# Perceiver block with soft mixture of experts on one core: score order, row fetches, turned logit rows and turning banks rearranged

## What is computed

```
x = x + xattn(layernorm(x), ctx)   # cross attention, width 256, softmax over 4096 keys, then Wo
x = x + attn(layernorm(x))         # causal self attention, 16 heads of 16; heads 0 to 2 weighted by region
x = x + ffn(layernorm(x))          # soft mixture of experts: 64 experts, 32 slots each

# ffn
logits = x @ phi.T + b             # 1024 tokens x 2048 slots
D = softmax(logits, over the 32 slots of an expert)
C = softmax(logits, over the 64 experts)
X = clip(D.T @ x); X = tanh(norm(X)); Y = X @ expert_w + expert_b
out = C @ Y
```

## Time and profile before

| | us |
|---|---|
| three runs | 563.71, 567.41, 567.92 |
| median | 567.41 |
| profiled execution, own time | 567.7 |
| its span in the profile | 565.9 |
| TensorE busy in the span | 533.9 |
| VectorE, ScalarE, GpSimd busy | 363.3, 363.8, 361.7 |

### The profile page before, as it was taken

How to read it: one execution, slowest core, us unless ns; L and a number is a source line. 1 busy time by engine, 2 the same in 40 slices (tenths; PEclk the granted TensorE clock), 3 DMA queues, 4 the chain that set the end, 5 groups by cost and what they waited for, 6 DMA issues and landing times. The chain is left out here.

```text
span 565.9 us, 9355 instructions
## 1 busy us (share of the span) xinstructions
PE 533.9 (94%) x3256; PEld 414.5 (73%) x3256; DVE 363.3 (64%) x736; ACT 363.8 (64%) x1016; POOL 361.7 (64%) x282
## 2 busy tenths in 40 slices
PE   5898999999999999999898989889999999899998
PEld 4786888888888888777566656446555887578898
DVE  1785344564455345745776898686999998588340
ACT  2446765856584866873787886328999895666320
POOL 2775989659775784755559675243465899688500
PEclk9999999999999999999898999999999999999999
DMA  8463464675743733175139500400000643978110
GB/s 295 160 224 134 163 224 162 185 282 183 251 149 131 248 143 103 48 169 136 32 100 204 181 1 1 151 0 1 1 1 1 118 105 109 331 230 245 57 48 28
DMA packets 38669, 75.45 MB, mean 133 GB/s; under 512 B 3408, under 2 KB 27360, under 8 KB 37728
## 3 DMA queue, kind: packets, MB, share of 16 engines
q1 hardware_dynamic: 36864, 68.57, 39.6%
q10 hardware_dynamic: 1760, 6.30, 3.1%
HBM read 68.56 MB, written 6.30 MB: 132 GB/s over the span
## 5 line engine op out<-in xcount | busy, mean ns | idle before, releaser
L387 POOL TENSOR_TENSOR ctxT_lo<-front,ctxT_hi 128x1024 fp32r<-128x1024 f32 x32 | 76.9, 2408 | 46.2 <-ACT ctxT_hi L682 46.2
L503 PE MATMUL ps<-ctx_both,pT_hi 128*128 128x512 f32 x256 | 94.6, 409 | 1.9 <-DVE pT_lo L858 1.9
L392 POOL TENSOR_TENSOR ctx_both<-ctx_in,ctx_both 128x1024 fp32r<-128x1024 f32 x32 | 76.5, 2395 | 16.3 <-ACT ctx_both L687 16.3
L505 PE MATMUL ps<-ctx_both,pT_lo 128*128 128x256 f32 x256 | 71.9, 281 | 0.0
L1774 PE MATMUL ps<-front,turned 128*128 128x512 f32 x128 | 61.0, 605 | 0.3 <-PEq L1008 0.3
L850 DVE TENSOR_SCALAR_CACHE_REDUCE first<-ps,qbk 128x512 f32<-128x512 f32 x32 | 24.0, 750 | 55.5 <-PE ps L475 53.2
L706 ACT CAST pT_hi<-ps 128x512 fp32r<-128x512 f32 x64 | 34.0, 590 | 38.3 <-PE ps L487 38.3
L503 PEld LDWEIGHTS ps<-ctx_both,pT_hi 128*128 128x128 f32 x256 | 48.2, 188 | 13.1 <-DVE pT_lo L858 2.8
L858 DVE TENSOR_TENSOR pT_lo<-ps,pT_hi 128x512 fp32r<-128x512 f32 x64 | 41.1, 685 | 16.4 <-ACT pT_hi L706 16.4
L1919 ACT ACTIVATE comb<-comb,cneg 128x64 f32<-128x64 f32 x128 | 50.8, 411 | 0.0
L505 PEld LDWEIGHTS ps<-ctx_both,pT_lo 128*128 128x128 f32 x256 | 48.5, 190 | 0.1
(11 more groups left out here) (260 smaller groups left out, 1436.1 us busy)
## 6 DMA issues: line engine op xcount, KB each, us to landing
front<-in_ctx_turned_dram SPq DMA_DIRECT2D x32, 512.0 KB, 4.7
ctx_in<-in_ctx_dram SPq DMA_DIRECT2D x32, 512.0 KB, 3.5
back<-in_L_ffn_expert_w_dram SPq DMA_DIRECT2D x11, 1024.0 KB, 5.9
turned<-in_L_ffn_expert_w_dram SPq DMA_DIRECT2D x5, 1024.0 KB, 5.8
phi_piece<-in_phi_turned_dram ACTq DMA_DIRECT2D x8, 512.0 KB, 6.3
phi_less_dram<-phi_piece ACTq DMA_DIRECT2D x4, 512.0 KB, 3.1
front<-phi_less_dram SPq DMA_DIRECT2D x1, 2048.0 KB, 14.0
front<-in_L_ffn_expert_b_dram SPq DMA_DIRECT2D x4, 512.0 KB, 10.2
```

Of the source, the lines that this page charges most:

```text
L387: nc.gpsimd.tensor_tensor(ctxT_lo[:, n % RING, :, :], turned_in[:, n % SLOTS, :, :], ctxT_hi[:, n % RING, :, :].bitcast(F32), ALU.subtract ...
L392: nc.gpsimd.tensor_tensor(ctx_both[:, m % RING, :, 1, :], by_tile(m), ctx_both[:, m % RING, :, 0, :].bitcast(F32), ALU.subtract).then_inc( ...
L503: nc.tensor.matmul(pO[q][:], pT_hi[:, c % 2, q, cols], ctx_both[:, m % RING, j, :, :].rearrange("p k d -> p (k d)"), start=c == 0 and j == ...
L505: last = nc.tensor.matmul(pO[q][:, 0:D], pT_lo[:, c % 2, q, cols], ctx_both[:, m % RING, j, 0, :], start=False, stop=c == NCH - 1 and j == ...
```

## The change

1. SP: the store of piece 3 is issued at the end of the first block. In the second block the order becomes stack 2, stack 3, then for s = 4 to 7 "store s, stack s".
2. Self attention, TensorE: the scores of group 1 come before `project_v(0..2)`. VectorE: maxima of group 1 come before the values, `last_norm` between its parts 1 and 2. ScalarE: the copy of the turned normed rows moves from behind `transposed(0)` to between `exps(2, 1)` and `exps(2, 2)`.
3. Logits: `norm` of the last tiles at v = 1 in place of 2; both copies of the turned rows at v = 4 in place of 5.
4. Experts: the pieces of C for tiles 0 to 5 go round three banks (0, 1 and 5) in place of two. Bank 5 was the second bank of the turned inputs, which now have bank 4 alone, so `transpose_inputs(s)` waits for ScalarE's copy of s - 1 in place of s - 2. Tiles 6 and 7 stay with banks 0 and 1.

```diff
@@ cross_attention, sync
                 if s < 2:
                     stack_rows(sp, kept, qk_dram, q_rows, k_rows, s)
+            store_parts(sp, kept, qk_dram, parts(3), 3)
             sp.wait_ge(phi_out, 16 * (4 + 1))
@@ self_attention, sync
             stack_rows(sp, kept, qk_dram, *first_rows(kept), 2)
-            store_parts(sp, kept, qk_dram, parts_in(kept.first, 3), 3)
             stack_rows(sp, kept, qk_dram, *first_rows(kept), 3)
-            store_parts(sp, kept, qk_dram, parts[:, 0, :, :], 4)
             for s in range(4, 8):
-                if s < 7:
-                    store_parts(sp, kept, qk_dram, parts[:, s - 3, :, :], s + 1)
+                store_parts(sp, kept, qk_dram, parts[:, s - 4, :, :], s)
                 stack_rows(sp, kept, qk_dram, q_late, k_late, s)
@@ self_attention, tensor
             product_of_attended()
+            for part in range(3):
+                score(1, part)
             for s in range(3):
                 project_v(s)
-            for part in range(3):
-                score(1, part)
@@ self_attention, scalar
                     exps(i + 2, 1)
+                    if i == 0:
+                        act.wait_ge(h2T_mm, B)
+                        nc.scalar.copy(hT[:, :, LAST * S:B * S], split_halves(psX[:])).then_inc(h2T_a, 1)
                     exps(i + 2, 2)
                 ...
                 transposed(i)
-                if i == 0:
-                    act.wait_ge(h2T_mm, B)
-                    nc.scalar.copy(hT[:, :, LAST * S:B * S], split_halves(psX[:])).then_inc(h2T_a, 1)
@@ self_attention, vector
             last_sums()
+            maxima(1, 0)
+            maxima(1, 1)
+            last_norm()
+            maxima(1, 2)
             values(0)
             values(1)
-            last_norm()
+            invert_sums(1, 0)
             values(2)
-            maxima(1, 0)
-            maxima(1, 1)
-            maxima(1, 2)
-            invert_sums(1, 0)
+            invert_sums(1, 1)
             maxima(2, 0)
-            invert_sums(1, 1)
@@ soft_moe
-        psL, psT, psE, psC = bank[0:4], bank[4:6], bank[6:8], bank[0:2]
+        psL, psT, psE, psC = bank[0:4], bank[4], bank[6:8], (bank[0], bank[1], bank[5])
+        def turn_bank(c, k):
+            return psC[(LB * c + k) % 3 if c < TT - 2 else k % 2]
@@ transpose_combine
-                    at_least(pe, cTlo_v, LB * c + k - 1)
+                    at_least(pe, cTlo_v, LB * c + k - (2 if c < TT - 2 else 1))
@@ transpose_inputs
-                at_least(pe, xT_a, s - 1)
+                at_least(pe, xT_a, s)
@@ soft_moe, tensor
-                if s < 2:
-                    pe.wait_ge(clip_v, 2 * s + 2)
+                if s == 0:
+                    pe.wait_ge(clip_v, 2)
@@ soft_moe, scalar
-                if v == LB + 1:
+                if v == LB:
                     act.wait_ge(pro_mm, 2)
@@ soft_moe, vector
-                if v == 2:
+                if v == 1:
                     dve.wait_ge(rstd_g, 2)
                     norm(TT - QT, TT)
-                if v == LB + 1:
+                if v == LB:
                     dve.wait_ge(pro_mm, 1)
```

More of the change, by code:

```diff
@@ L1794, in transpose_combine @@
                     pe.wait_ge(cmul_g, LB * c + k + 1)
-                    at_least(pe, cTlo_v, LB * c + k - 1)
+                    at_least(pe, cTlo_v, LB * c + k - (2 if c < TT - 2 else 1))
                     for j in range(4):
-                        last = nc.tensor.transpose(psC[k % 2][:, j * P:(j + 1) * P],
+                        last = nc.tensor.transpose(turn_bank(c, k)[:, j * P:(j + 1) * P],
                                                    comb[:, c, (4 * k + j) * P:(4 * k + j + 1) * P], ident[:])
@@ L1802, in transpose_inputs @@
                 pe.wait_ge(tanh_a, s + 1)
-                at_least(pe, xT_a, s - 1)
+                at_least(pe, xT_a, s)
                 for c in range(DH):
-                    last = nc.tensor.transpose(psT[s % 2][:, c * P:(c + 1) * P], xh[:, s % 2, c * P:(c + 1) * P], ident[:])
+                    last = nc.tensor.transpose(psT[:, c * P:(c + 1) * P], xh[:, s % 2, c * P:(c + 1) * P], ident[:])
                 last.then_inc(xT_mm, 1)
@@ L1928, in combine_out @@
                     act.wait_ge(cT_mm, LB * c + k + 1)
-                    nc.scalar.copy(comb_hi[c][:, k * 512:(k + 1) * 512], psC[k % 2][:]).then_inc(cT_a, 1)
+                    nc.scalar.copy(comb_hi[c][:, k * 512:(k + 1) * 512], turn_bank(c, k)[:]).then_inc(cT_a, 1)
             def outputs_high(s):
@@ L1974, in _ @@
                 at_least(act, e_mm, s - 1)
-                nc.scalar.copy(xhT[:, s % 2, :, :].rearrange("p c s -> p (c s)"), psT[s % 2][:, 0:DH * P]).then_inc(xT_a, 1)
+                nc.scalar.copy(xhT[:, s % 2, :, :].rearrange("p c s -> p (c s)"), psT[:, 0:DH * P]).then_inc(xT_a, 1)
                 if turned_at(s) is not None:
@@ L2084, in combine_low @@
                     dve.wait_ge(cT_a, LB * c + k + 1)
-                    nc.vector.tensor_tensor(comb_lo[:, c, cols], psC[k % 2][:], comb_hi[c][:, cols].bitcast(F32),
+                    nc.vector.tensor_tensor(comb_lo[:, c, cols], turn_bank(c, k)[:], comb_hi[c][:, cols].bitcast(F32),
                                             ALU.subtract).then_inc(cTlo_v, 1)
```

## The result

The changed kernel took 560.47 us in the median of 4 runs (556.28 to 560.81), the kernel before beside it 565.83; the ratio is 0.9869, with a 95% interval of 0.9820 to 0.9917. So it is faster by 1.3 to 1.5%, 5.4 to 8.7 us by the medians. The profiled execution took 560.81 us, span 559.0, against 567.7 and 565.9 before. The forecast was 557.0, range 553 to 562. The sum behind it was 10.8 us, though, and the two spans differ by 6.9: this needs an account by stages. Runs in the chip's slower state are left out of all medians here: one of ten of no1, and the profiled one of sp_old_late (762 us at a mean granted clock of 0.66), which therefore has no usable trace.

The account below looks back on a forecast made before the run. TensorE was taken as the bound: 533.9 of 565.9 us at work, about 32 standing. Gains 3.1 + 0 + 5.5 + 2.2 = 10.8 from 567.7 gave 556.9 (556.6 by the median), stated as 557.0, range 553.0 to 562.0.

Parts of the forecast that it names:

- Part 2: Self attention: scores of group 1 ahead of the values start `project_qk(4)` 3.1 us earlier; ends 1.5 and 3.5.
- Part 1: SP's store order: rows 4 and 5 come without a wait, but the stall only moves; gain 0, ends 0 and 1.9.
- 1.33 + 0.62: Self attention: the stall before `score(8, 0)` moves to before L1250 and keeps this length in us.
- Part 3: Logits: turned rows a unit sooner bring `logit(10)` 5.5 us earlier; ends 2.5 and 5.9.
- the three things in the rows: Logits: a 1.35 us wait for the norm, 2.55 for the copy, 1.7 for a slow unit; together 5.6.
- the 0.3 for unit 4: Logits: TensorE would lose 0.3 us waiting for unit 4's early inputs, which want a division on GpSimd.
- The rival with VectorE as the bound: Logits: VectorE takes the place of the waits, gain there 2.5 us, total 7.8, time 559.9; chance 0.12.
- The rival of the clock: Logits: small TensorE stops lower the clock, 1.7 us more per unit; 573.9 us with ten slow units; chance 0.03.
- the stretch that I held against it: Logits, 400 to 440 us: clock 1.00 with TensorE busy 40.00 of 40 us, cited against the clock falling.
- Part 4: Experts: three banks for the pieces of C end step 7 2.2 us earlier; ends 0.5 and 2.7.
- its first two rivals: VectorE bounds the logits (559.9 us, chance 0.12); experts stay bound by ScalarE or the weights (560 us, chance 0.09).
- the lower ends: Smallest gains of the four parts; the prediction summed them to 5 to 6 us, giving 562.

Follow-up runs that it names:

- no1: The changed kernel with all SP edits undone (store 3 late, each store of 4 to 7 ahead of the stack before it); median 558.67 us.
- sp_old_late: The changed kernel with store 3 still early but stores and stacks of 4 to 7 in the old order; median 555.35 us.
- sp_7: The changed kernel with store 7 alone issued ahead of stack 6; median 555.35 us.
- no4: The changed kernel with two banks again for the pieces of C and two for the turned inputs; median 561.78 us.
- new_again: The changed kernel run once more, unchanged; median 557.87 us, ratio 0.9851 to the kernel before.
- no2: The changed kernel with group 1's scores behind the values again, ScalarE's copy and VectorE's order also undone; median 559.42 us.
- warm: The changed kernel with twenty transposes of the identity on TensorE ahead of its first weights; median 555.24 us.
- no3: The changed kernel with the turned rows of the logits a unit later again; median 561.95 us.
- warm_before: The kernel before with twenty transposes of the identity on TensorE ahead of its first weights; median 563.93 us, ratio 0.9952.

## Why the prediction was right, point by point

**Part 2** was right in mechanism and close in size. `score(2, 0)` came 2.07 us sooner (forecast 2.0), `project_qk(4)` 3.59 (forecast 3.1), ScalarE's copy is the last thing TensorE waits for there, 0.77. The term was a little small, as the earlier store of 3 inside it is worth 1.6 by no1 and not 1.2.

**Part 1** is where a step of the argument failed: "Rows 6 and 7 keep their distance, as everything they hang on moves along." They do not; the fetch of 7 now stands behind a store that is itself behind the fetch of 6. The lead of 3.6 us was 2.9 at `project_qk(7)` (a wait of 0.24 on VectorE), 2.5 at L1248 and 1.8 at `score(10, 0)`, where the rows are waited for, and 2.5 reached the logits, as some small waits behind it went. In sp_7 the lead is 3.6 at `score(10, 0)` (53.59 for 57.17) and 4.2 at the logits. The rest of the step held: the wait of 1.33 for rows 4 and 5 is gone, it bought nothing, and the wait ahead of L1248 came out at 2.00, for 1.33 + 0.62 = 1.95. My value of 0 for this part was too good by some 0.6 in the profiled pair (2.5 for 3.1 at the logits), and by sp_7 the order for the last pieces costs 0.9 to 3.1 in the self attention against a better one, though whole runs at an equal clock differ by 0.5 only.

**Part 3** was forecast at 5.5 and measured at 6.0, by undoing it as well. The sum of the three things in the rows was 5.6: the two waits and the slow unit of the earlier trace rows all went, and the 0.3 for unit 4 was not lost. Counted by the starts of the logits the three gave more than their brackets: `logit(5)` comes 1.57 sooner (for 1.35), `logit(8)` another 2.82 (for 2.55) and `logit(9)` another 1.70. The clock stood at 1.00 from 377 on. The rival with VectorE as the bound did not come: TensorE has no wait from 377 to 470, while VectorE is at 37.60 of 40 us, as in the earlier trace rows. The rival of the clock did not come either; the stretch that I held against it has no stop of TensorE in it, so it told nothing of small stops.

**Part 4** was forecast at 2.2. Steps 4 to 7 gained 1.96 and the steps behind them 0.50, 2.46 together; that TensorE would merely keep its gain from step 8 on missed one place, step 14. Its turned inputs were followed by the eight transposes of C only 0.52 us later and with stops inside them (1.22 for eight, 522.23 and 522.75 in the trace of before); after, it is 0.22 and 1.04, and with two banks again, in no4, the 0.50 is back. The waits fell to 1.8 in five:

```profile
479.09 0.63 PE L1799 MATMUL ps<-ident,comb 128*128 128x128 f32 x4 [0.41 <-DVE comb_lo L2087]
...
481.73 0.63 PE L1799 MATMUL ps<-ident,comb 128*128 128x128 f32 x4 [0.40 <-DVE comb_lo L2087]
...
483.25 0.63 PE L1799 MATMUL ps<-ident,comb 128*128 128x128 f32 x4 [0.24 <-DVE comb_lo L2087]
```

The first two, in step 5, answer to 0.67 and 0.50 in the earlier trace rows; the third is in step 6. The single bank for the turned inputs costs nothing where it stands alone, in steps 0 to 3: 11.32 for 11.31. I did not run it without the third bank.

**The total.** 2.5 + 6.0 + 2.5 = 11.0 for a sum of 10.8, but from one execution against another, and partly by luck: parts 3 and 4 gave 0.5 and 0.3 more than their terms, the self attention 0.6 less. The median of 560.5 alone could not have told the forecast from its first two rivals, at 559.9 and 560; the stages do, as part 3 gave 6.0 and not 2.5, and part 4 2.5 and not 0.5. One sum in the prediction is wrong: the lower ends, 1.5, 0, 2.5 and 0.5, make 4.5 and 563.2, not 5 to 6 and 562. The time came in at 560.5 and 557.9, above the 557.0 and inside the range, because the first profiled execution, and probably two runs beside it, lost 4.1 at the start, and because the gain of 10.8 contained clock. In 45 runs of before, ten had a mean granted clock of 1.00 and took 563.6 to 564.7; the others, at 0.991 to 0.994, took 565.5 to 570.5. Two runs of the new kernel had 1.00 and took 556.28 and 555.06. Among such runs the change is thus worth about 8.5 us. These means do not see the start, though: two runs of no1 say 1.00 as well and took 560.8, two others 555.9 and 556.3. I had given the slow clock behind the long stop its 1.7 us of gain without saying that not every execution of before has to pay it. That is argued from the means of whole runs; no trace of before at 1.00 was taken.

## What to carry to other kernels

Where a stop is removed, follow the resource with a rhythm of its own past the next two or three waits. Here SP's loop of store, landing and fetch takes 7 us per piece against 5.1 to 5.8 of work, so a lead won upstream dries up there; issue a store ahead of the fetch of the piece before, so that it lands while that fetch is under way. And compare stage by stage, undoing one part at a time: logits and experts agreed within 0.15 us between traces where whole runs differed by 5 to 8.

## What the runs showed of the hardware that I had not expected

**The start at either level.** The same first product took 3.4 to 3.8 us or 1.99, and the lower level lasted up to about 10 us in most traces and up to the first score at 20.69 in one. The Trainium skill, "TensorE: Matmul & The Clock Gate", in "Part 1: The HAM clock gate", says that the number of slow matmuls at a kernel's start varies between runs of the same kernel. The traces agree with that, by the lengths: in two executions of the same kernel the first score stands at 16.53 (new_again) and 20.69 (after).

**The same stop, two outcomes.** Seven executions stand 2.00 us ahead of the product at L1248 (L1250 or L1251 in some). Behind it the product took 3.52, 3.68 and 3.65 in three of them (after, no2, warm; granted clock 0.54 in after) and 1.99 in four (no3, no4, sp_7, new_again; 1.00 in new_again). The row of after stands in the section on the result; the same place in new_again, the same kernel:

```profile
304.85 1.99 PE L1248 MATMUL ps<-w_proj,h1T 128*128 128x256 f32 x8 [2.00 <-DVE wide L1424]
...
315.54 0.58 PE L1198 MATMUL ps<-more 96*128 96x128 bf16 x4 [3.41 <-DMA more<-qk_parts_dram]
```

The 1.5 us saved at L1248 are simply waited for at the rows, 3.41 for 0.93, where the rows also came 0.8 us later. So one trace does not price the clock behind a stop of this length. The longer one of 2.55, for the turned rows, was followed by the full loss in all three traces that have it (before, no3, warm_before: logits of 110.37 to 110.41).

**Fetches that a load behind them does not slow.** 1.5 MB in rows turned over through DRAM took 12 us, with or without a 2 MB load behind them. The load took 8.1 us on its own and 13.7 behind the fetches.
